# Routing two expert layers: gate logits from the residual stream itself instead of from its normed copy

## The reference

```python
def _layernorm(x, eps=1e-05):
    return (x - mean(x)) / sqrt(var(x) + eps)
def _moe(t, Wg, bg, w1, w2):            # t: (4096, 256), 8 experts, 2 of them per token
    logits = t @ Wg.T + bg
    topw, topi = top_k(softmax(logits), 2)
    topw = topw / sum(topw)
    gate, up = split(t @ w1[e].T)       # 256 columns each, for each chosen expert e
    return sum over the two experts of topw * (silu(gate) * up) @ w2[e].T
x = x + _moe(_layernorm(x), ...)        # applied twice, after retention and after the recurrence
```

## Time and profile before

| what | value |
|---|---|
| median of three timed runs | 1308.2 us (1307.96 to 1311.38) |
| time of the profiled execution | 1312.09 us |
| its span in the trace | 1310.3 us |
| TensorE, VectorE, ScalarE, GpSimd busy | 85%, 65%, 46%, 45% |
| mean granted TensorE clock | 0.927 |
| first routing stage, block start to first gather issued | 273.9 to 322.16 us |
| second routing stage, block start to first gather issued | 1032.5 to 1080.12 us |

### The profile page before, as it was taken

One profiled execution on the slowest core, in us unless ns is written; L12 is line 12 of the kernel. 1 busy time (PEld: TensorE's weight loads), 2 busy tenths in 40 slices (PEclk: granted clock), 3 DMA queues, 4 the chain that ended last, 5 costly groups with the idle time before them and its releaser, 6 DMA issues. The chain is left out here.

```text
span 1310.3 us, 35896 instructions
## 1 busy us (share of the span) xinstructions
PE 1112.6 (85%) x14261; PEld 819.7 (63%) x14261; DVE 854.6 (65%) x1843; ACT 601.8 (46%) x1281; POOL 595.9 (45%) x602
## 2 busy tenths in 40 slices
PE   6999999873999995679999989989886749999960
PEld 3778787662888884235555555555555437888850
DVE  4677766668555555566978877697663585555546
ACT  4666666333333332263755737466562333333323
POOL 4556565221677774406144151624410206777740
PEclk9999999986999998699999999999996869999985
DMA  8342320068433332000110101010000492333338
GB/s 293 133 154 81 115 83 34 2 221 313 163 101 104 103 104 90 33 33 4 34 35 3 34 3 34 4 34 3 3 2 3 160 363 89 105 102 104 102 127 330
DMA packets 50686, 125.72 MB, mean 96 GB/s; under 512 B 7648, under 2 KB 26848, under 8 KB 47712
## 3 DMA queue, kind: packets, MB, share of 16 engines
q1 hardware_dynamic: 36896, 86.20, 18.4%
q0 software_dynamic: 13632, 37.24, 9.0%
HBM read 79.63 MB, written 43.78 MB: 94 GB/s over the span
## 5 line engine op out<-in xcount | busy, mean ns | idle before, releaser
L1135 POOL DMA_INDIRECT ffn_xs<-xn_rows,ffn_from_row x142 | 138.2, 973 | 123.3 <-DVE ffn_second_y_at L1511 80.6
L1143 POOL DMA_INDIRECT y_rows<-ffn_ys,ffn_to_row x142 | 140.0, 986 | 59.2 <-issue 34.8
L1539 DVE TENSOR_TENSOR ffn_act_in<-ffn_silu_g,ffn_ps_h 128x256 f32<-128x256 f32 x142 | 59.8, 421 | 153.3 <-ACT ffn_silu_g L1177 153.3
L1290 PE MATMUL ffn_ps_h<-ffn_w_high,ffn_xst 128*128 x568 | 156.6, 398 | 0.7 <-issue 0.7
L1177 ACT ACTIVATE ffn_silu_g<-ffn_ps_h 128x256 f32<-128x256 f32 x142 | 54.5, 384 | 217.6 <-PE ffn_ps_h L1290 217.6
L1311 PE MATMUL ffn_ps_o<-ffn_w,ffn_act_t 128*128 x852 | 134.1, 293 | 0.0
L1311 PEld LDWEIGHTS ffn_ps_o<-ffn_w,ffn_act_t 128*128 128x128 f32 x852 | 109.3, 189 | 0.4 <-issue 0.2
L1876 POOL TENSOR_TENSOR rec_mixed_k<-rec_mixed_k,rec_xnt 128x512 f32<-128x512 f32 x16 | 17.4, 1089 | 199.4 <-DVE rec_mixed_k L2664 199.4
L1290 PEld LDWEIGHTS ffn_ps_h<-ffn_w_high,ffn_xst 128*128 128x128 f32 x568 | 97.4, 190 | 13.6 <-issue 1.2
L726 DVE TENSOR_TENSOR ret_probs<-ret_score,ret_causal 128x2048 f32<-128x2048 f32 x32 | 73.3, 2292 | 31.0 <-PE ret_score L573 31.0
L1290 PE MATMUL ffn_ps_h<-ffn_w_low,ffn_xst 128*128 x284 | 89.8, 398 | 0.0
(11 more groups left out here) (360 smaller groups left out, 2858.7 us busy)
## 6 DMA issues: line engine op xcount, KB each, us to landing
home<-y_rows SPq DMA_DIRECT2D x30, 512.0 KB, 4.9
w_split<-home SPq DMA_DIRECT2D x24, 512.0 KB, 3.7
ffn_w_high<-w_split SPq DMA_DIRECT2D x8, 1024.0 KB, 8.4
ffn_w_low<-w_split SPq DMA_DIRECT2D x8, 1024.0 KB, 10.7
ffn_w<-w_split SPq DMA_DIRECT2D x8, 1024.0 KB, 14.3
home<-in_f_w SPq DMA_DIRECT2D x12, 512.0 KB, 5.8
xn_rows<-home SPq DMA_DIRECT2D x12, 512.0 KB, 11.5
out<-x SPq DMA_DIRECT2D x8, 512.0 KB, 5.9
```

What stands on the lines that cost most here:

```text
L1135: pool.indirect_dma_start(xs[:, n % SLOTS, :], None, xn_rows[:], bass.IndirectOffsetOnAxis(ap=from_row[:, n:n + 1], axis=0)) \
L1143: pool.indirect_dma_start(y_rows[:], bass.IndirectOffsetOnAxis(ap=to_row[:, m:m + 1], axis=0), ys[:, m % SLOTS, :], None).then_inc(ys_stor ...
L1290: mm = pe.matmul(ps_h[:, u % 2, :], one_pass(xst[:, n % 3, part, k, :]), one_pass(w1[w_part][k][:, bass.ds(e, E_COLUMNS)]), start=(part + ...
L1539: dve.tensor_tensor(act_in[:, n % 3, :], silu_g[:, u % 2, :], ps_h[:, u % 2, FF:2 * FF], ALU.mult) \
```

## The change

Five edits in `experts()`, which act in both of its runs:

- TensorE transposes `x` itself instead of `xn`, into `xt` with five places. The gate's weights are centred instead: a matmul with a matrix of 1/256 gives each expert's mean weight (`gate_means`), and VectorE subtracts it. The product with a token's row of `x` then needs only that token's `rstd`, which VectorE multiplies in after the logits have been transposed back; the bias is added by an operation of its own.
- The identity matrix has one tensor for the whole program, loaded once at its start, and leaves the constants of the route and of the recurrence.
- TensorE's wait for the constants moves from its head into `gate_means`, and the wait for the moments and the eleven transposes of the identity are gone.
- VectorE norms steps 0 to 5; ScalarE norms steps 6 and 7 by `rstd * x + offset`, and VectorE makes `offset = -mean * rstd` for it.
- SyncE waits for the last two steps on a semaphore of ScalarE's.

```diff
+        X_PLACES = 5
...
-        ident, tri_f, b_gate, rank_of = (constants[:, at[n]] for n in ("ident", "tri", "f_b_gate", "rank_of"))
+        tri_f, b_gate, rank_of = (constants[:, at[n]] for n in ("tri", "f_b_gate", "rank_of"))
...
-        w_gate = constants[:, at["f_w_gate"]].rearrange("p (k c) -> p k c", k=KT)
+        w_gate_raw = constants[:, at["f_w_gate"]].rearrange("p (k c) -> p k c", k=KT)
+        w_gate = sb("w_gate", [P, KT, 32])
...
-                xnt = stage_sb("xnt", [P, 4, KT, UNROLL * P])
+                xt = stage_sb("xt", [P, X_PLACES, KT, UNROLL * P])
                 logits_t = stage_sb("logits_t", [P, UNROLL * P])
+                one_of_c = logits_t[:, 0:P]
...
         STEPS = TILES // UNROLL
+        XN_STEPS = STEPS - 2
...
                 for n in range(STEPS):
-                    sp.wait_ge(xn_ready, n + 1)
+                    if n < XN_STEPS:
+                        sp.wait_ge(xn_ready, n + 1)
+                    else:
+                        sp.wait_ge(last_xn_ready, n - XN_STEPS + 1)
                     sp.dma_start(xn_rows.rearrange("(i p) c -> p i c", p=P)[:, n * UNROLL:(n + 1) * UNROLL, :],
                                  xn_of[n]).then_inc(xn_stored, 16)
...
             def _(pool):
+                pool.memset(one_of_c, 1.0 / C).then_inc(means_filled, 1)
...
+                def take_logits(n):
+                    act.wait_ge(logits_t_in_psum, n + 1)
+                    if n >= 1:
+                        act.wait_ge(logits_in_psum, n)
+                    act.activation(logits_t[:], ps_l[:], ACT.Copy).then_inc(logits_t_ready, 1)
...
+                def norm(n):
+                    for j in range(UNROLL):
+                        i = n * UNROLL + j
+                        at_j = i - XN_STEPS * UNROLL
+                        op = act.activation(xn_of[n][:, j, :], x[:, i, :], ACT.Identity, bias=offset[:, at_j:at_j + 1],
+                                            scale=rstd[:, i:i + 1])
+                    op.then_inc(last_xn_ready, 1)
+
                 for n in range(STEPS):
                     act.wait_ge(xt_in_psum, n + 1)
-                    if n >= 4:
-                        act.wait_ge(logits_t_in_psum, n // 4)
-                    act.activation(xnt[:, n % 4, :, :], ps_xt[n % 2][:], ACT.Copy).then_inc(xnt_ready, 1)
-                    if n % 4 == 3:
-                        act.wait_ge(logits_t_in_psum, n // 4 + 1)
-                        if n >= 4:
-                            act.wait_ge(logits_in_psum, n // 4)
-                        act.activation(logits_t[:], ps_l[:], ACT.Copy).then_inc(logits_t_ready, 1)
+                    if n >= X_PLACES:
+                        act.wait_ge(logits_t_in_psum, 1)
+                    act.activation(xt[:, n % X_PLACES, :, :], ps_xt[n % 2][:], ACT.Copy).then_inc(xt_ready, 1)
+                    if n == 4:
+                        take_logits(0)
+                act.wait_ge(ln_offset, 2)
+                norm(XN_STEPS)
+                take_logits(1)
+                norm(XN_STEPS + 1)
...
-                pe.wait_ge(consts_loaded, 32)
-
-                def transpose_norm(n):
-                    pe.wait_ge(xn_ready, n + 1)
+                def transpose_step(n):
                     if n >= 2:
-                        pe.wait_ge(xnt_ready, n - 1)
+                        pe.wait_ge(xt_ready, n - 1)
                     for j in range(UNROLL):
                         for k in range(KT):
                             mm = pe.transpose(ps_xt[n % 2][:, k, j * P:(j + 1) * P],
-                                              xn_of[n][:, j, k * P:(k + 1) * P], ident[:])
+                                              x[:, n * UNROLL + j, k * P:(k + 1) * P], ident[:])
                     mm.then_inc(xt_in_psum, 1)
 
+                def gate_means():
+                    pe.wait_ge(consts_loaded, 32)
+                    pe.wait_ge(means_filled, 1)
+                    for k in range(KT):
+                        mm = pe.matmul(ps_a[:, 0:32], one_of_c, w_gate_raw[:, k, :], start=(k == 0), stop=(k == KT - 1))
+                    mm.then_inc(gate_means_in_psum, 1)
+
                 def gate_logits(n):
 
-                    pe.wait_ge(xnt_ready, 4 * n + 4)
+                    pe.wait_ge(xt_ready, 4 * n + 4)
+                    pe.wait_ge(gate_ready, 1)
                     if n >= 1:
                         pe.wait_ge(logits_t_ready, n)
                     for k in range(KT):
                         for h in range(4):
-                            mm = pe.matmul(ps_l[32 * h:32 * h + 32, :], w_gate[:, k, :], xnt[:, h, k, :],
+                            mm = pe.matmul(ps_l[32 * h:32 * h + 32, :], w_gate[:, k, :], xt[:, (4 * n + h) % X_PLACES, k, :],
                                            start=(k == 0), stop=(k == KT - 1))
                     mm.then_inc(logits_t_in_psum, 1)
...
-                pe.wait_ge(ln_moments, MOMENT_STEPS)
-                keep_going(ps_o[:, 1, :], 11)
                 for n in range(STEPS):
-                    transpose_norm(n)
-                    if n % 4 == 0 and n > 0:
-                        gate_logits(n // 4 - 1)
-                    if n % 4 == 2 and n > 2:
-                        transpose_logits(n // 4 - 1)
+                    transpose_step(n)
+                    if n == 2:
+                        gate_means()
+                    if n == 4:
+                        gate_logits(0)
+                    if n == 6:
+                        transpose_logits(0)
                 gate_logits(ROUNDS - 1)
                 transpose_logits(ROUNDS - 1)
...
-                for n in range(STEPS):
+                def norm(n):
                     dve.wait_ge(ln_rstd, sum(first <= n for first in ROOTS))
...
                         i = (4 * n + h) * UNROLL
                         op = dve.tensor_tensor(logits[:, i:i + UNROLL, :],
                                                ps_o[:, n, :].rearrange("p (j r) -> p j r", j=UNROLL)[:, :, 32 * h:32 * h + NE],
-                                               b_gate[:].unsqueeze(1).to_broadcast([P, UNROLL, NE]), ALU.add)
-                    op.then_inc(logits_ready, 1)
+                                               rstd[:, i:i + UNROLL].unsqueeze(2).to_broadcast([P, UNROLL, NE]), ALU.mult)
+                    op.then_inc(logits_scaled, 1)
+                    dve.wait_ge(logits_scaled, n + 1)
+                    dve.tensor_tensor(logits[:, half, :], logits[:, half, :],
+                                      b_gate[:].unsqueeze(1).to_broadcast([P, TILES // ROUNDS, NE]), ALU.add) \
+                        .then_inc(logits_ready, 1)
                     dve.wait_ge(logits_ready, n + 1)
...
+                norm(0)
+                norm(1)
+                dve.wait_ge(gate_means_in_psum, 1)
+                dve.tensor_tensor(w_gate[:], w_gate_raw, ps_a[:, 0:32].unsqueeze(1).to_broadcast([P, KT, 32]), ALU.subtract) \
+                    .then_inc(gate_ready, 1)
+                for n in range(2, XN_STEPS):
+                    norm(n)
+                late = slice(XN_STEPS * UNROLL, TILES)
+                dve.wait_ge(ln_rstd, len(ROOTS) - 1)
+                dve.tensor_tensor(offset[:], mean[:, late], rstd[:, late], ALU.mult).then_inc(ln_offset, 1)
+                dve.wait_ge(ln_offset, 1)
+                dve.tensor_scalar(offset[:], offset[:], -1.0, None, ALU.mult).then_inc(ln_offset, 1)
+
+                dve.wait_ge(consts_loaded, 32)
+                ranks = rank_of[:].unsqueeze(1).to_broadcast([P, TILES // ROUNDS, NE])
+                for n in range(ROUNDS):
+                    choose(n)
...
-F_ROUTE = (("ident", P), ("tri", P), ("rank_of", NE), ("fills", TILES), ("count", P), ("part_no", 1), ("spill", NTILES))
+F_ROUTE = (("tri", P), ("rank_of", NE), ("fills", TILES), ("count", P), ("part_no", 1), ("spill", NTILES))
...
-B_SHAPES = (("ident", P), ("same_head", P), ("one_of", 4), ("earlier", 64), ("same_in_pair", 2 * HD), ("head_mean", P))
+B_SHAPES = (("same_head", P), ("one_of", 4), ("earlier", 64), ("same_in_pair", 2 * HD), ("head_mean", P))
...
+        ident = ctx.enter_context(nc.sbuf_tensor("ident", [P, P], F32))
```

32 lines of the change are left out of this document (18 added, 14 removed).

## The result

| | before | after | ratio |
|---|---|---|---|
| first series, medians of 14 runs each | 1308.75 us (1304.54 to 1317.41) | 1303.24 us (1296.42 to 1310.41) | 0.9948 [0.9932, 0.9964] |
| second series, 31 and 8 runs | 1306.68 us (1301.81 to 1315.6) | 1300.13 us (1297.45 to 1308.71) | 0.9941 [0.9912, 0.9969] |

The account below looks back on a forecast made before the run. Each routing stage was taken as one chain, so its head's saving reaches the end unless a DMA is late: 12.95 - 2 x 1.0 (gathers) = 10.95 us, off 1308.2 gives 1297.3 us; own range 1295 to 1299.5, whole range 1294.0 to 1303.0.

Parts of the forecast that it names:

- the rivals at 1301: Gathers standing behind all weights (1301.2 us, 15%) and a low clock at the head (1301.3 us, 10%).
- gathers of over 5 us: Sign that would show the forecast wrong; gathers of tiles 0 and 1 were to land in 3 to 4.5 us.
- Head: Start of each routing stage, to the end of the choice: 6.25 us saved in the second, 6.7 in the first.
- VectorE would be nearly as late as TensorE: At the second choice: VectorE's first choice ends at T+15.7, 0.3 us before the second can start.
- The clock: Rival at the head: three transpose steps at half clock cost 2.0 us a stage, 1301.3 us; 10%.
- Gathers: First gathers of each stage, issued with loads still running: 1.0 us lost a stage, between bounds 0 and 4.0.
- the row of small packets: Trace row of the loads, 2762 packets of 0.051 us each: six packets ahead of a gather are 0.3 us.
- turns: At the gathers: time lost beside a load is packet turns, so 4.0 us are six packets of 0.69 us.
- The row: Trace of gathers beside another load: 6.7 us instead of 2.7, giving the upper bound of 4.0 us.
- the gather behind all weights: Rival: tile 1's gather lands with the last weights, 3.5 us saved a stage, 7 in both, 1301.2 us; 15%.
- the estimate from it: At the gathers, from the skill page: one to two turns cost 0.5 to 1.7 us for each stage.

Follow-up runs that it names:

- c0: The changed kernel itself, unaltered, run again beside three further versions: 1300.13 us, ratio to before 0.9941.
- a3: The changed kernel with VectorE norming all eight steps and ScalarE none: 1306.53 us, ratio to before 0.9977.
- b1: The changed kernel with second weights (1 KB records) loaded first and the first weights' low half (8 KB records) last: 1305.84 us, one execution.
- c1: The changed kernel with each load of the second weights cut into four of 256 KB, same records: 1303.96 us, ratio to before 0.9965.

## Why the prediction was half right

The time fell inside the stated range, but only because the range was drawn to take in the rivals at 1301. The forecast's own mechanism was right for the head and wrong for the gathers, and by its own sign (gathers of over 5 us) the prediction had failed there.

**Head: right, and 1 us too careful.** Forecast: transposes at T+0.1, first choice at T+11.0, second at T+16.0, end at T+20.7. Measured in the second stage: T+0.00, 10.6, 15.3, 20.0. Saved are 7.1 and 6.9 us, 14.0 in both, against 12.95. The gate's centring was in time, VectorE had no gap above 0.3 us before either choice (0.54 in c0's second stage, where the clock was low), the stores were not waited for, and step 7 was normed by T+16.5 (forecast 17.35). That VectorE would be nearly as late as TensorE is what a3 shows.

**The clock: mostly right.** In the profiled execution it was 1.00. Of eleven executions with the new head seven show 3.4 us at half clock from about T+1 on, in one of their two stages; b1, second stage (window, columns as in the earlier trace rows):

```profile
1029.30:1032.00 2.70, 2.70 (x16) 2.55 (x14) 1.91 (x6) 1.67 (x3) 2.70 (x3) 0.50 0.95 332
```

This moves the end of the choice from T+20.0 to 21.2. The rival had priced 2.0 us for both stages of every execution; it comes as 1.2 us in some, and the gathers hide half of it: in c0 `hidden(0)` is 0.6 us later in the stage that has it.

**Gathers: the term that failed.** "The bounds are 0 and 4.0. I take 1.0, near the row of small packets, since more packets can stand ahead than six." Measured are 3.7 and 3.4 us between the gain at the issue of the first gather (7.6 and 6.7) and the gain at the first expert matmul (3.9 and 3.3). The choice between the bounds was made by the size of a packet, that is, by taking the lost time for turns. b1 and c1 take that away: same latency with records eight times as long and loads a quarter as large. The row was the nearer one, and it shows the same thing when its window is drawn tight: beside that load of 16 KB records 1.1 MB pass with hardly a packet of q0. DMA view before, 346.4 to 349.6:

```profile
q1 hardware_dynamic: 70, 1.12, 99.9%
q0 software_dynamic: 8, 0.00, 0.1%
```

The rival that came true in the number, the gather behind all weights, has the mechanism only in part: a gather waits behind about 1 MB and then shares the engines. Its 3.5 us a stage are met by 3.9 and 3.3, since only 0.4 to 0.5 MB more was left. The Trainium skill (DMA: Bandwidth & Descriptors, section "Queues, rings and completion order") has an engine change queues after a packet of 9 to 17 descriptors; the estimate from it was 0.5 to 1.7 us. The measurement differs and decides: the silence of q0 is as long in bytes at 8 KB records as at 1 KB, 1.0 MB in b1 and in after, where packets of a fixed number of records would have made it eight times longer. Whether the queues take turns after it, these views don't tell.

With 3.9 + 3.3 = 7.2 us instead of 10.95 the sum would have given 1301.0 from the median of 1308.2. The timed savings are 6.8 and 7.7 us. The agreement is in part luck, as the last paragraph shows.

**What the error rests on.** I had read the DMA queue at its end, two windows wide, and not over the stage. 17 MB at 98.6% of 16 engines are a path of 48 us by itself, and the first expert matmul came 49.2 and 49.4 us after T. From this one row the ceiling follows: before, `hidden(0)` was at T+53.3 and 52.4, so with these loads in this order no more than some 4 us a stage could be had at the start of the loop, whatever the head saved.

**Not settled.** By the last `output` the two blocks of the profiled executions save 1.08 + 3.15 = 4.2 us, and those of c0 2.74 + 1.50 = 4.2 us, less than the 7.2 at their starts and than the 6.8 and 7.7 timed. What the loops give back is known: stops and the lower clock, as above. In after's first loop it is 2.8 us, of which 1.7 are the longer stop behind the recurrence's weights; in c0's second it is 1.1, for which the clock alone accounts with 1.2. What the timed runs have beyond 4.2 us is not located. From the last `output` of the first block to the start of the second, the fourteen profiled executions took between 516.4 and 527.8 us, and both ends are executions of the changed kernel. So the medians of many runs carry the verdict, and single profiles only the mechanism.
